# Decoder layer on Trainium2: the feed-forward's row maximum by one reduction over 2048 columns in the next tile, in place of four over 512

## Chip, cores and metric

The kernel runs on one core of one Trainium2 chip. The metric is the device time of one execution in microseconds (us); smaller is better. Where several executions were timed, their median is given.

## What is computed

One decoder layer on 8 sequences of 256 tokens with 512 channels: attention, then a long convolution over a context, then a feed-forward, each on the layer-normalised stream and added to it. The change touches the feed-forward alone, whose weights are 512 x 2048, 512 x 2048 and 2048 x 512:

```python
def activation_quant(x):
    scale = 127.0 / jnp.clip(jnp.max(jnp.abs(x), axis=-1, keepdims=True), EPS, None)
    return jnp.clip(jnp.round(x * scale), -128.0, 127.0) / scale
...
gate = bit_linear(x, w_gate)
up = bit_linear(x, w_up)
activated = up * jnp.square(jax.nn.relu(gate))
activated = subln(activated, subln_weight)      # x * rsqrt(mean(x^2) + 1e-6) * g
return bit_linear(activated, w_down)            # quantises its input's rows to 8 bits
```

`bit_linear` rounds its input, row by row, to integers of -128 to 127, scaled by the greatest absolute value of the row, and its weights to -1, 0, 1. So the 2048 activations of a row have to be finished, weighed by `g`, before their greatest value, and with it the integers for the last product, is known.

## The kernel before

The work has three stages: attention (0 to some 305 us), the convolution (to some 460 us), and the feed-forward, which runs over 16 tiles of 128 rows. Each engine has its own instruction list, in an order written by hand; they meet at semaphores alone. `schedule` (L966) lays out one `turn` per tile: turns 0 to 3 written out, turns 4 to 13 as a loop over pairs, then turns 14 and 15. A turn is a software pipeline. Turn t does the gate and up products of tile t, the end of the scaling and the quantising of tile t-1, the product with `w_down` of tile t-2, and prepares the rows of tile t+2.

The 2048 hidden columns of a tile are done in four chunks of 512 (`IC` = 4). For chunk n of tile t:

- TensorE (L1069) does 4 products for the gate and 4 for the up projection into PSUM;
- ScalarE (`relu`, L1093 and L1095) makes relu(gate) squared;
- VectorE (`chunk`, L1189) multiplies that by the up projection into the small tile `a` (named `toep` in the trace, whose memory it uses again);
- GpSimd (`weigh`, L1306) multiplies by `g` into `act_w` (named `big`), and ScalarE (`square`, L1104) sums the squares of `a`;
- VectorE (`greatest`, L1193) takes the greatest absolute value of the 512 weighed columns into one column of `mb4`.

With all four chunks done, VectorE sums the squares (`scale`, L1199 to L1204), reduces `mb4` to `mb` (L1206), GpSimd raises the variance to -0.5 (`power`, L1302), and VectorE makes the scale `qs` from it (`scale_b`, L1211 to L1219). ScalarE then scales all 2048 columns (`quantise`, L1112), GpSimd makes them integers in bfloat16 (`integers`, L1314), a DMA on SyncE's queue transposes them (L1000), and TensorE multiplies them by `w_down` (L1057); VectorE adds the residual (`final`, L1227).

VectorE's turn also holds the steps of tile t+2: `rows_x2` (L1138, adds the convolution's part to the stream), `rows_stats` (L1143), `rows_mean` (L1148), `rows_var` (L1152), `rows_norm` (L1156), `rows_greatest` (L1160), `rows_scale` (L1164 to L1171), `rows_int` (L1175 to L1179). `rows_stats` and `rows_mean` have an `apart` ahead, an empty instruction between the wait and the work.

What waits for what, in a turn: TensorE's chunk 2 waits for VectorE's chunk 0, its chunk 3 for VectorE's chunk 1, and chunks 0 and 1 of the next tile for VectorE's chunks 2 and 3. ScalarE's `square` of chunk 0 waits until VectorE has summed the squares of the tile before (L1199). ScalarE's order is relu 0, relu 1, square 0, relu 2, square 1, rows_out, relu 3, square 2, quantise (of tile t-1), square 3.

The names of the chunks in what follows: chunk n is VectorE's product of chunk n, L1189, and square n is ScalarE's L1104 of it.

Of the kernel before, what the change touches and what calls it, by code (L numbers as in the profile page):

```python
# [23 lines left out]
ALU = mybir.AluOpType  # L24
ACT = mybir.ActivationFunctionType
AX = mybir.AxisListType
# [5 lines left out]
P = 128  # L32
B, T, C = 8, 256, 512
# [15 lines left out]
NT = B * TT  # L49
# [18 lines left out]
def wait(eng, signal, turn, n):  # L68
    eng.wait_ge(signal.sem, signal.at(turn, n))
# [829 lines left out]
def ffn(nc, ctx, m, g, out, multiply, add_up):  # L899
# [5 lines left out]
    def sb(name, shape, dt=F32):  # L905
        return ctx.enter_context(nc.sbuf_tensor(name, shape, dt))

    def two(name, shape, dt=F32):
        return [sb(f"{name}{r}", shape, dt) for r in range(2)]

    def sig(name, per=1):
        return Signal(ctx.enter_context(nc.semaphore("f_" + name)), per)

    IC = FF // C
# [18 lines left out]
    rl, r2 = ([kv[:, r * C:(r + 1) * C] for r in range(2)] for kv in (kv0, kv1))  # L933
    a = [t[:] for t in toep]
    asq, ss = sb("asq", [P, C]), sb("ss", [P, IC])
    act_w = [m.big[:, 0:FF], m.big[:, FF:2 * FF]]
    act32 = m.big[:, 2 * FF:3 * FF]
    act8 = [y.bitcast(BF16)[:, 0:FF] for y in ys]
    act8t = two("act8t", [P, FK, P], BF16)
    mb4 = sb("mb4", [P, IC])  # L940
    cc, sm, var, r4, cr, mb, bm, rb, qs = (sb(n, [P, 1]) for n in (
        "cc", "sm", "var", "r4", "cr", "mb", "bm", "rb", "qs"))
    fd = two("fd", [P, 1])
# [9 lines left out]
        "turned", "x2", "bn", "mv", "ve", "rs", "xn"))  # L953
    s_mx, s_cl, s_rc, s_s127, s_cx, s_cx2, s_cf = (sig(n) for n in ("mx", "cl", "rc", "s127", "cx", "cx2", "cf"))
    s_x32, s_xq, s_xqt, s_xqe = (sig(n) for n in ("x32", "xq", "xqt", "xqe"))
    s_g, s_u, s_rl, s_r2, s_a, s_as, s_w, s_mb4 = (sig(n, IC) for n in ("g", "u", "rl", "r2", "a", "as", "w", "mb4"))
    s_sm, s_cc, s_var, s_r4, s_mb, s_cr, s_bm, s_rb, s_qs, s_fd = (sig(n) for n in (
        "sm", "cc", "var", "r4", "mb", "cr", "bm", "rb", "qs", "fd"))
    s_a32, s_a8, s_dn, s_fin = (sig(n) for n in ("a32", "a8", "dn", "fin"))
# [172 lines left out]
    def vector(dve):  # L1132
# [3 lines left out]
        def rows_x2(t, bank=TB):  # L1136
            wait(dve, s_turned, t, 1)
            nc.vector.tensor_tensor(row(t), bank, row(t), ALU.add).then_inc(s_x2.sem, 1)  # L1138

        def rows_stats(t):  # L1140
            wait(dve, s_x2, t, 1)
            apart(dve)
            nc.vector.bn_stats(st[:], row(t)).then_inc(s_bn.sem, 1)  # L1143

        def rows_mean(t):
            wait(dve, s_bn, t, 1)
            apart(dve)
            nc.vector.bn_aggr(mv[:], st[:]).then_inc(s_mv.sem, 1)  # L1148

        def rows_var(t):  # L1150
            wait(dve, s_mv, t, 1)
            nc.vector.tensor_scalar(ve[:], mv[:, 1:2], LN_EPS, None, ALU.add).then_inc(s_ve.sem, 1)  # L1152

        def rows_norm(t):
            wait(dve, s_rs, t, 1)
            nc.vector.tensor_scalar(xn, row(t), mv[:, 0:1], rs[:], ALU.subtract, ALU.mult).then_inc(s_xn.sem, 1)  # L1156

        def rows_greatest(t):
            wait(dve, s_xn, t, 1)
            nc.vector.tensor_reduce(mx[:], xn, AX.X, ALU.max, apply_absolute_value=True).then_inc(s_mx.sem, 1)  # L1160

        def rows_scale(t):
            wait(dve, s_mx, t, 1)
            nc.vector.tensor_scalar(cl[:], mx[:], Q_EPS, None, ALU.max).then_inc(s_cl.sem, 1)  # L1164
            wait(dve, s_cl, t, 1)
            nc.vector.reciprocal(rc[:], cl[:]).then_inc(s_rc.sem, 1)
            nc.vector.tensor_scalar(cx[:], cl[:], 1.0 / 127.0, None, ALU.mult).then_inc(s_cx.sem, 1)
            wait(dve, s_rc, t, 1)
            nc.vector.tensor_scalar(s127[:], rc[:], 127.0, None, ALU.mult).then_inc(s_s127.sem, 1)
            wait(dve, s_cx, t, 1)  # L1170
            nc.vector.tensor_scalar(cx2[:], cx[:], cx[:], w3[:], ALU.mult, ALU.mult).then_inc(s_cx2.sem, 1)  # L1171

        def rows_int(t, r):
            wait(dve, s_s127, t, 1)
            nc.vector.tensor_scalar(xq32, xn, s127[:], MAGIC, ALU.mult, ALU.add).then_inc(s_x32.sem, 1)  # L1175
            wait(dve, s_cx2, t, 1)
            nc.vector.tensor_scalar(cf_all[:, bass.ds(t, 1)], cx2[:], cx[:], None, ALU.mult).then_inc(s_cf.sem, 1)
            wait(dve, s_x32, t, 1)
            nc.vector.tensor_scalar(xq[r][:], xq32, -MAGIC, None, ALU.add).then_inc(s_xq.sem, 1)  # L1179

        def chunk(t, n, after=True):
            wait(dve, s_r2, t, n + 1)
            wait(dve, s_u, t, n + 1)
            if n >= 2 or after:

                tp, np_ = (t, n - 1) if n >= 2 else (t - 1, n - 1 + IC)
                wait(dve, s_as, tp, np_)
                wait(dve, s_w, tp, np_)
            nc.vector.tensor_tensor(a[n % 2][:], UB[:, n % 2, :], r2[n % 2][:], ALU.mult).then_inc(s_a.sem, 1)  # L1189

        def greatest(t, n, r):
            wait(dve, s_w, t, n + 1)
            nc.vector.tensor_reduce(mb4[:, n:n + 1], act_w[r][:, n * C:(n + 1) * C], AX.X, ALU.max,  # L1193
                                    apply_absolute_value=True).then_inc(s_mb4.sem, 1)

        def scale(t, r):
            cf = cf_all[:, bass.ds(t, 1)]
            wait(dve, s_as, t, IC)
            nc.vector.tensor_reduce(sm[:], ss[:], AX.X, ALU.add).then_inc(s_sm.sem, 1)  # L1199

            nc.vector.tensor_scalar(cc[:], cf, cf, 1.0 / FF, ALU.mult, ALU.mult).then_inc(s_cc.sem, 1)
            wait(dve, s_cc, t, 1)
            wait(dve, s_sm, t, 1)
            nc.vector.tensor_scalar(var[:], sm[:], cc[:], SUB_EPS, ALU.mult, ALU.add).then_inc(s_var.sem, 1)  # L1204
            wait(dve, s_mb4, t, IC)
            nc.vector.tensor_reduce(mb[:], mb4[:], AX.X, ALU.max).then_inc(s_mb.sem, 1)  # L1206

        def scale_b(t, r):
            cf = cf_all[:, bass.ds(t, 1)]
            wait(dve, s_r4, t, 1)  # L1210
            nc.vector.tensor_scalar(cr[:], r4[:], cf, None, ALU.mult).then_inc(s_cr.sem, 1)  # L1211
            wait(dve, s_mb, t, 1)
            wait(dve, s_cr, t, 1)
            nc.vector.tensor_scalar(bm[:], mb[:], cr[:], Q_EPS, ALU.mult, ALU.max).then_inc(s_bm.sem, 1)
            wait(dve, s_bm, t, 1)
            nc.vector.reciprocal(rb[:], bm[:]).then_inc(s_rb.sem, 1)
            wait(dve, s_rb, t, 1)
            nc.vector.tensor_scalar(qs[:], rb[:], cr[:], 127.0, ALU.mult, ALU.mult).then_inc(s_qs.sem, 1)
            nc.vector.tensor_scalar(fd[r][:], bm[:], m.wmean[:, 2:3], 1.0 / 127.0, ALU.mult, ALU.mult  # L1219
                                    ).then_inc(s_fd.sem, 1)  # L1220

        def final(t, r, stores):
            wait(dve, s_dn, t, 1)
            wait(dve, s_fd, t, 1)
            if stores is not None:
                dve.wait_ge(d_o[r].sem, stores * 16)
            nc.vector.scalar_tensor_tensor(ot[r][:], DB, fd[r][:], row(t), ALU.mult, ALU.add).then_inc(s_fin.sem, 1)  # L1227

        def turn(t, r, after=True, last=True, rows=True, more=True, stored=True, pair=None):
            chunk(t, 0, after)  # L1230
            if not after:
                rows_norm(t + 1)
                rows_greatest(t + 1)
                rows_scale(t + 1)
            if rows:
                rows_x2(t + 2)
            if after:
                greatest(t - 1, 3, 1 - r)
            if rows:
                rows_stats(t + 2)  # L1240
            chunk(t, 1, after)
            if not after:
                rows_int(t + 1, 1 - r)
            if after:
                scale(t - 1, 1 - r)
            if rows:
                rows_mean(t + 2)
            if after:
                scale_b(t - 1, 1 - r)
            if rows:  # L1250
                rows_var(t + 2)
            greatest(t, 0, r)
            chunk(t, 2)
            greatest(t, 1, r)
            if rows:
                rows_norm(t + 2)
            chunk(t, 3)
            if rows:
                rows_greatest(t + 2)
                rows_scale(t + 2)  # L1260
            greatest(t, 2, r)
            if rows:
                rows_int(t + 2, r)
            if last:
                final(t - 2, r, pair - 1 if stored else None)
# [24 lines left out]
        rows_mean(1)  # L1290
        rows_var(1)
        schedule(turn, dve.Fori)
        greatest(NT - 1, 3, 1)
        scale(NT - 1, 1)
        scale_b(NT - 1, 1)
        for t in (NT - 2, NT - 1):
            final(t, t % 2, NT // 2 - 1)

    def gpsimd(pool):
# [38 lines left out]
        integers(NT - 1, 1)  # L1338

    return sync, tensor, scalar, vector, gpsimd  # L1340


# [90 lines left out]
```

## Time and profile before

| what | value |
|---|---|
| median of 3 runs | 678.32 us (677.24 to 678.36) |
| the profiled execution | 679.29 us, its span 677.5 us |
| TensorE busy | 613.7 us, 91% of the span |
| VectorE busy | 485.3 us, 72% |
| ScalarE busy | 455.3 us, 67% |
| GpSimd busy | 269.8 us, 40% |
| mean granted TensorE clock | 0.965 |

The span is the time from the first to the last instruction of the profiled execution; 1.8 us of that execution's time lie around it. Busy shares are means over three stages that are limited by different things, so what the change is worth has to be read in the feed-forward alone, in the last third of the span.

### The profile page before, as it was taken

Reading aid. Unit: us, or ns where it says so; the run is one execution under the profiler, and the core shown is the slowest. Engines: PE = TensorE matmul, PEld = TensorE weight load, DVE = VectorE, ACT = ScalarE, POOL = GpSimd, SP = SyncE. Lnnn points to the kernel's source line nnn. Section 1 sums busy time; section 2 is a strip of 40 time slices with the busy share of each in tenths; the row PEclk is TensorE's granted clock in tenths of the full one; section 3 lists DMA queues with packets and bytes.
Section 4 is the critical chain, followed back from the end, with each engine's and each line's share of the span. In section 5 each row is a group of like instructions: output and inputs, shape, how many; then the busy total and the mean of one; then the engine's idle time right before and its main releaser. Section 6 shows DMA issues by size and latency. Waiting matters only on the chain.

```text
span 677.5 us, 10465 instructions
## 1 busy us (share of the span) xinstructions
PE 613.7 (91%) x2818; PEld 342.0 (50%) x2818; DVE 485.3 (72%) x949; ACT 455.3 (67%) x799; POOL 269.8 (40%) x248
## 2 busy tenths in 40 slices
PE   5889999999999999989999999957799999899975
PEld 4525454535454543367777777743344444444432
DVE  3455767575758372437778877898999999999961
ACT  2363666666666667158988888864778778688771
POOL 1000000100010001137777777742566666666671
PEclk9959999999999997989999999987999999999997
DMA  8473144536261717026555656431042342432424
GB/s 312 126 207 85 40 105 145 122 126 138 110 176 71 208 41 178 24 79 193 169 169 171 192 170 174 156 110 44 16 109 63 82 105 62 106 79 62 94 48 108
DMA packets 75589, 80.89 MB, mean 119 GB/s; under 512 B 38000, under 2 KB 49776, under 8 KB 75440
## 3 DMA queue, kind: packets, MB, share of 16 engines
q1 hardware_dynamic: 75568, 80.65, 43.1%
q8 instruction: 9, 0.15, 0.1%
q14 instruction: 12, 0.10, 0.0%
HBM read 47.51 MB, written 4.28 MB: 76 GB/s over the span
## 4 chain that ended last, share of the span: by engine, by line
PE 26%; DVE 16%; issue 7%; POOL 3%; ACT 2%; DVEq 1%; DMA 1%; ACTq 0%; POOLq 0%; SPq 0%
PE ps L708 20%; DVE toep L1189 3%; PE ps L1069 3%; PE ps L1057 2%; DVE mb L1193 2%; POOL big L1306 2%; DVE ps L1175 1%; DVE ps L1156 1%; DVE mx L1160 1%; DVE qo L761 1%; POOL r L1302 1%; ACT asq L1104 1%; DMA act8t<-ys 1%; ACT kv L1093 1%; DVE x_all L1138 1%
## 5 line engine op out<-in xcount | busy, mean ns | idle before, releaser
L708 PE MATMUL ps<-kv,toep 128*128 128x288 f32 x640 | 157.3, 409 | 1.1 <-PEq L1368 1.1
L708 PEld LDWEIGHTS ps<-kv,toep 128*128 128x128 f32 x640 | 122.3, 192 | 36.1 <-issue 2.4
L1069 PE MATMUL ps<-wt,xqt 128*128 128x512 bf16 x512 | 123.4, 387 | 17.3 <-DVE toep L1189 16.5
L1306 POOL TENSOR_TENSOR big<-toep,wst 128x512 f32<-128x512 f32 x64 | 82.9, 1295 | 41.9 <-DVE toep L1189 41.9
L396 ACT ACTIVATE big<-ps,kscale 128x512 f32<-128x512 f32 x128 | 85.5, 696 | 12.7 <-PE ps L246 10.3
L1069 PEld LDWEIGHTS ps<-wt,xqt 128*128 128x128 bf16 x512 | 48.5, 99 | 79.1 <-DVE toep L1189 24.2
L246 PE MATMUL ps<-qx,kx 128*128 128x512 f32 x128 | 78.3, 633 | 10.5 <-ACT big L396 8.6
L761 DVE TENSOR_REDUCE qo<-big 128x2048 f32 (+1 forms) x32 | 72.2, 2258 | 0.0
L1057 PE MATMUL ps<-wt,act8t 128*128 128x512 bf16 x256 | 60.3, 390 | 7.9 <-DMA act8t<-ys 7.0
L696 POOL TENSOR_TENSOR kv<-ctx 128x768 f32<-128x768 f32 (+1 forms) x32 | 52.7, 1648 | 36.7 <-PE ps L708 27.9
L750 DVE TENSOR_TENSOR big<-ps,qd 128x1024 f32<-128x1024 f32 x32 | 39.2, 1224 | 37.1 <-ACT ys L840 34.6
L1104 ACT ACTIVATE asq<-toep 128x512 f32<-128x512 f32 x64 | 39.5, 618 | 38.8 <-DVE sm L1199 37.4
L217 PE MATMUL ps<-wq_s,xt 128*128 128x512 f32 x128 | 63.4, 593 | 0.8 <-ACT xt L360 0.8
L550 DVE RECIPROCAL yt<-ps 128x512 f32<-128x512 f32 x16 | 53.6, 3349 | 14.4 <-PE ps L264 14.4
L800 POOL TENSOR_TENSOR big<-ys,qd 128x768 f32<-128x768 f32 x32 | 56.6, 1768 | 13.8 <-ACT ys L840 11.7
L284 PE MATMUL ps<-wo_s,yt 128*128 128x512 f32 x128 | 56.6, 594 | 1.0 <-DVE yt L555 1.0
L246 PEld LDWEIGHTS ps<-qx,kx 128*128 128x128 f32 x128 | 25.5, 204 | 46.4 <-ACT big L396 26.2
L646 POOL COPY vo<-vn 128x256 f32<-128x256 f32 x8 | 3.2, 398 | 112.5 <-PE ps L273 86.3
L1189 DVE TENSOR_TENSOR toep<-ps,kv 128x512 f32<-128x512 f32 x64 | 43.5, 679 | 4.7 <-ACT kv L1095 3.4
L1057 PEld LDWEIGHTS ps<-wt,act8t 128*128 128x128 bf16 x256 | 25.2, 100 | 40.9 <-DMA act8t<-ys 8.7
L1193 DVE TENSOR_REDUCE mb<-big 128x1 f32<-128x512 f32 x64 | 43.3, 676 | 0.2 <-POOL big L1306 0.2
L1095 ACT ACTIVATE kv<-kv 128x512 f32<-128x512 f32 x64 | 40.3, 630 | 2.0
(118 smaller groups left out, 958.9 us busy)
## 6 DMA issues: line engine op xcount, KB each, us to landing
qx<-kv SPq DMA_DIRECT2D x128, 128.0 KB, 2.4
wst<-in_wall SPq DMA_DIRECT2D x12, 1024.0 KB, 6.4
wst<-in_wall SPq DMA_DIRECT2D x48, 256.0 KB, 3.7
toep<-krows SPq DMA_DIRECT2D x32, 256.0 KB, 3.7
ctx<-in_ctxt SPq DMA_DIRECT2D x32, 192.0 KB, 2.6
out_y<-ot SPq DMA_DIRECT2D x16, 256.0 KB, 2.9
conv_part<-qo SPq DMA_DIRECT2D x14, 256.0 KB, 2.7
x_all<-in_x SPq DMA_DIRECT2D x2, 1536.0 KB, 14.5
```

The lines of the kernel that those rows point to most:

```text
L217: mm = pe.matmul(bank[:, t, :], xt[:, k, t * P:(t + 1) * P], wq_s[:, k, :], start=(k == 0), stop=(k == CK - 1))
L246: pe.matmul(SB[:, n % 2, :], kx[:, kv, s * P:(s + 1) * P].bitcast(F32R), qx[:, kv, gp * C:(gp + 1) * C].bitcast(F32R), start=True, stop=Tr ...
L284: mm = pe.matmul(OB[:, t, :], yt[:, k, t * P:(t + 1) * P], wo_s[:, k, :], start=(k == 0), stop=(k == CK - 1))
L396: act.activation(pt[:, s, kv, gp * C:(gp + 1) * C], SB[:, n % 2, :], ACT.Exp, scale=kscale[:, c:c + 1]).then_inc(s_e.sem, 1)
L708: mm = pe.matmul(m.ps[:, LB * r + lb, :].rearrange("p (b s) -> p b s", s=WIDE)[:, :, 0:PAIRS], m.toep[r][:, d * P:(d + 1) * P], m.kv[r][:, ...
L761: nc.vector.tensor_reduce(qo[:, :, bass.ds(h * HD, HD)], z[r][:], AX.X, ALU.add).then_inc(s_red.sem, 1)
L800: nc.gpsimd.tensor_tensor(z[r][:, :, :, HD - SHIFTS:HD].rearrange("p n j s -> p n s j"), window(ys[r][:], SHIFTS - 1, (SHIFTS * EW, NB), ( ...
L1057: mm = pe.matmul(DB, act8t[r][:, k, :], down_w[:, k, :], start=(k == 0), stop=(k == FK - 1))
L1069: mm = pe.matmul(bank[:, n % 2, :], xqt[r][:, k, :], wt[:, k, n * C:(n + 1) * C], start=(k == 0), stop=(k == CK - 1))
L1189: nc.vector.tensor_tensor(a[n % 2][:], UB[:, n % 2, :], r2[n % 2][:], ALU.mult).then_inc(s_a.sem, 1)
L1193: nc.vector.tensor_reduce(mb4[:, n:n + 1], act_w[r][:, n * C:(n + 1) * C], AX.X, ALU.max, apply_absolute_value=True).then_inc(s_mb4.sem, 1)
L1306: nc.gpsimd.tensor_tensor(act_w[r][:, n * C:(n + 1) * C], a[n % 2][:], gb[:, n * C:(n + 1) * C], ALU.mult).then_inc(s_w.sem, 1)
```

## The change

The four maxima over 512 columns become one over 2048. It is taken in the turn of the next tile, after the steps `scale`, `rows_mean` and `rows_var` and ahead of `scale_b`. The second reduction from `mb4` to `mb`, the tile `mb4` and its semaphore go. `rows_var` now stands ahead of `scale_b`.

```diff
-        def greatest(t, n, r):
-            wait(dve, s_w, t, n + 1)
-            nc.vector.tensor_reduce(mb4[:, n:n + 1], act_w[r][:, n * C:(n + 1) * C], AX.X, ALU.max,
-                                    apply_absolute_value=True).then_inc(s_mb4.sem, 1)
+        def greatest(t, r):
+            wait(dve, s_w, t, IC)
+            nc.vector.tensor_reduce(mb[:], act_w[r], AX.X, ALU.max, apply_absolute_value=True).then_inc(s_mb.sem, 1)
...
             nc.vector.tensor_scalar(var[:], sm[:], cc[:], SUB_EPS, ALU.mult, ALU.add).then_inc(s_var.sem, 1)
-            wait(dve, s_mb4, t, IC)
-            nc.vector.tensor_reduce(mb[:], mb4[:], AX.X, ALU.max).then_inc(s_mb.sem, 1)
...
             if rows:
                 rows_x2(t + 2)
-            if after:
-                greatest(t - 1, 3, 1 - r)
             if rows:
                 rows_stats(t + 2)
             chunk(t, 1, after)
...
                 scale(t - 1, 1 - r)
             if rows:
                 rows_mean(t + 2)
-            if after:
-                scale_b(t - 1, 1 - r)
             if rows:
                 rows_var(t + 2)
-            greatest(t, 0, r)
+            if after:
+                greatest(t - 1, 1 - r)
+                scale_b(t - 1, 1 - r)
             chunk(t, 2)
-            greatest(t, 1, r)
             if rows:
                 rows_norm(t + 2)
             chunk(t, 3)
             if rows:
                 rows_greatest(t + 2)
                 rows_scale(t + 2)
-            greatest(t, 2, r)
             if rows:
                 rows_int(t + 2, r)
...
         schedule(turn, dve.Fori)
-        greatest(NT - 1, 3, 1)
+        greatest(NT - 1, 1)
         scale(NT - 1, 1)
         scale_b(NT - 1, 1)
```

The other engines' orders are as before. Three places of VectorE's order move.

The first is in the loop, between chunk 0 and chunk 1; `st` are the statistics of tile t+2, REGISTER_ALU rows count the loop's semaphore values. Before:

```order
L1138 TENSOR_TENSOR x_all<-ps,x_all 128x512
L1193 TENSOR_REDUCE mb4<-big 128x1 [waits f_w]
L1143 BN_STATS st<-x_all 128x6 [waits f_x2]
L69 REGISTER_ALU
L1189 TENSOR_TENSOR toep1<-ps,kv1 128x512 [waits f_as,f_w,f_u,f_r2]
```

and with the change:

```order
L1137 TENSOR_TENSOR x_all<-ps,x_all 128x512
L1142 BN_STATS st<-x_all 128x6 [waits f_x2]
L69 REGISTER_ALU
L1188 TENSOR_TENSOR toep1<-ps,kv1 128x512 [waits f_as,f_w,f_u,f_r2]
```

The maximum of the last chunk no longer stands between the sum `x_all` and the statistics that wait for it.

The second is in the loop, between chunk 1 and chunk 2 (`cr` is the first instruction of `scale_b`, `fd` its last, `ve` is `rows_var`). Before:

```order
L1204 TENSOR_SCALAR var<-sm,cc 128x1 [waits f_sm,f_cc]
L1206 TENSOR_REDUCE mb<-mb4 128x1 [waits f_mb4]
L1148 BN_AGGR mv3<-st 128x2 [waits f_bn]
L1211 TENSOR_SCALAR cr<-r4,cf_all 128x1 [waits f_r4]
L1214 TENSOR_SCALAR bm<-mb,cr 128x1 [waits f_cr,f_mb]
L1216 RECIPROCAL rb<-bm 128x1 [waits f_bm]
L1218 TENSOR_SCALAR qs<-rb,cr 128x1 [waits f_rb]
L1219 TENSOR_SCALAR fd0<-bm,wmean 128x1
L1152 TENSOR_SCALAR ve<-mv3 128x1 [waits f_mv]
L1193 TENSOR_REDUCE mb4<-big 128x1 [waits f_w]
L69 REGISTER_ALU
L1189 TENSOR_TENSOR toep0<-ps,kv1 128x512 [waits f_as,f_w,f_u,f_r2]
```

and with the change:

```order
L1202 TENSOR_SCALAR var<-sm,cc 128x1 [waits f_sm,f_cc]
L1147 BN_AGGR mv3<-st 128x2 [waits f_bn]
L1151 TENSOR_SCALAR ve<-mv3 128x1 [waits f_mv]
L1192 TENSOR_REDUCE mb<-big 128x1 [waits f_w]
L1207 TENSOR_SCALAR cr<-r4,cf_all 128x1 [waits f_r4]
L1210 TENSOR_SCALAR bm<-mb,cr 128x1 [waits f_cr,f_mb]
L1212 RECIPROCAL rb<-bm 128x1 [waits f_bm]
L1214 TENSOR_SCALAR qs<-rb,cr 128x1 [waits f_rb]
L1215 TENSOR_SCALAR fd0<-bm,wmean 128x1
L69 REGISTER_ALU
L1188 TENSOR_TENSOR toep0<-ps,kv1 128x512 [waits f_as,f_w,f_u,f_r2]
```

The maximum over 2048 columns now stands between `var` and `cr`, which waits for GpSimd's power of `var`, and `ve` stands right behind the `mv3` that it needs.

The third is the end of VectorE's program, behind chunk 3 of the last tile. Before:

```order
L1189 TENSOR_TENSOR toep1<-ps,kv1 128x512 [waits f_as,f_w,f_u,f_r2]
L1193 TENSOR_REDUCE mb4<-big 128x1 [waits f_w]
L1227 SCALAR_TENSOR_TENSOR ot1<-ps,fd1,x_all 128x512 [waits f_d_o1,f_fd,f_dn]
L1193 TENSOR_REDUCE mb4<-big 128x1 [waits f_w]
L1199 TENSOR_REDUCE sm<-ss 128x1 [waits f_as]
```

and with the change:

```order
L1188 TENSOR_TENSOR toep1<-ps,kv1 128x512 [waits f_as,f_w,f_u,f_r2]
L1223 SCALAR_TENSOR_TENSOR ot1<-ps,fd1,x_all 128x512 [waits f_d_o1,f_fd,f_dn]
L1192 TENSOR_REDUCE mb<-big 128x1 [waits f_w]
L1197 TENSOR_REDUCE sm<-ss 128x1 [waits f_as]
```

There the long maximum stands in the open, ahead of the scaling of the last tile.

## Rows read from the trace of the kernel before

**Rows 1.** One turn of the loop: busy time of each engine, granted clock, DMA.

```profile
core 0: us, PE busy (x) PEld busy (x) DVE busy (x) ACT busy (x) POOL busy (x), PEclk, DMA share, GB/s
582.85:595.18 12.33, 11.36 (x58) 5.31 (x57) 11.54 (x33) 9.50 (x19) 8.15 (x7) 1.00 0.36 85
```

**Rows 2.** Who waited for whom from 508.9 to 620.5 us, nine turns: total, times, longest.

```profile
PE ps L1069 <- DVE toep L1189: 8.7, 18, 0.7
DVE cr L1211 <- POOL r L1302: 4.6, 9, 0.5
```

**Rows 3.** VectorE in order of time, one turn: start us, us, line, operation [idle before].

```profile
576.41 0.68 DVE L1189 TENSOR_TENSOR toep<-ps,kv 128x512 f32<-128x512 f32 x1
...
579.83 0.15 DVE L1206 TENSOR_REDUCE mb<-mb 128x1 f32<-128x4 f32 x1
...
580.57 0.21 DVE L1211 TENSOR_SCALAR cr<-r,cf_all 128x1 f32<-128x1 f32 x1 [0.51 <-POOL r L1302]
...
581.60 0.14 DVE L1152 TENSOR_SCALAR ve<-mv 128x1 f32<-128x1 f32 x1
581.66 0.67 DVE L1193 TENSOR_REDUCE mb<-big 128x1 f32<-128x512 f32 x1
582.25 0.68 DVE L1189 TENSOR_TENSOR toep<-ps,kv 128x512 f32<-128x512 f32 x1
...
588.75 0.68 DVE L1189 TENSOR_TENSOR toep<-ps,kv 128x512 f32<-128x512 f32 x1
```

**Rows 4.** VectorE in order of time, where the convolution ends and the feed-forward starts.

```profile
449.46 0.68 DVE L1138 TENSOR_TENSOR x_all<-ps,x_all 128x512 f32<-128x512 f32 x1
450.25 0.69 DVE L1143 BATCH_NORM_STATS2 st<-x_all 128x6 f32<-128x512 f32 x1
...
452.43 0.16 DVE L1148 BATCH_NORM_AGGREGATE mv<-st 128x2 f32<-128x6 f32 x1
452.65 0.15 DVE L1152 TENSOR_SCALAR ve<-mv 128x1 f32<-128x1 f32 x1
452.76 2.29 DVE L761 TENSOR_REDUCE qo<-big 128x256 f32<-128x2048 f32 x1
454.96 0.80 DVE L1156 TENSOR_SCALAR ps<-x_all,mv,rs 128x512 f32<-128x512 f32 x1
...
467.78 0.69 DVE L1143 BATCH_NORM_STATS2 st<-x_all 128x6 f32<-128x512 f32 x1 [0.49 <-DVE x_all L1138]
```

**Rows 5.** ScalarE in order of time, same turn: square 2, and the next turn's relu 0.

```profile
583.67 0.61 ACT L1104 ACTIVATE asq<-toep 128x512 f32<-128x512 f32 x1
...
587.49 0.63 ACT L1095 ACTIVATE kv<-kv 128x512 f32<-128x512 f32 x1
```

**Rows 6.** The transposing DMA's issue, its landing, and TensorE's first product with it.

```profile
588.58 1.79 SPq L1000 DMA_TRANSPOSE act8t<-ys  x1
...
DMA to landing us min/median/max: 4.3/4.3/4.3
...
593.60 3.62 PE L1057 MATMUL ps<-wt,act8t 128*128 128x512 bf16 x16
```

**Rows 7.** The last two turns and the end, each engine in order of time.

```profile
638.06 0.68 DVE L1189 TENSOR_TENSOR toep<-ps,kv 128x512 f32<-128x512 f32 x1
...
653.49 0.68 DVE L1189 TENSOR_TENSOR toep<-ps,kv 128x512 f32<-128x512 f32 x1
...
646.00 7.07 PE L1069 MATMUL ps<-wt,xqt 128*128 128x512 bf16 x32
...
663.66 6.01 PE L1057 MATMUL ps<-wt,act8t 128*128 128x512 bf16 x16 [6.57 <-DMA act8t<-ys]
670.61 3.61 PE L1057 MATMUL ps<-wt,act8t 128*128 128x512 bf16 x16 [0.94 <-DVE ot L1227]
...
654.49 0.61 ACT L1104 ACTIVATE asq<-toep 128x512 f32<-128x512 f32 x1
...
665.08 1.77 SPq L1000 DMA_TRANSPOSE act8t<-ys  x1
```

More of the change, by code:

```diff
@@ L939, in ffn @@
     act8t = two("act8t", [P, FK, P], BF16)
-    mb4 = sb("mb4", [P, IC])
     cc, sm, var, r4, cr, mb, bm, rb, qs = (sb(n, [P, 1]) for n in (
@@ L955, in ffn @@
     s_x32, s_xq, s_xqt, s_xqe = (sig(n) for n in ("x32", "xq", "xqt", "xqe"))
-    s_g, s_u, s_rl, s_r2, s_a, s_as, s_w, s_mb4 = (sig(n, IC) for n in ("g", "u", "rl", "r2", "a", "as", "w", "mb4"))
+    s_g, s_u, s_rl, s_r2, s_a, s_as, s_w = (sig(n, IC) for n in ("g", "u", "rl", "r2", "a", "as", "w"))
     s_sm, s_cc, s_var, s_r4, s_mb, s_cr, s_bm, s_rb, s_qs, s_fd = (sig(n) for n in (
```

## The prediction

> **What bounds the kernel now.** The change touches only the feed-forward, so I first looked for a stretch of it that repeats. In the loop a turn takes 12.33 us, with VectorE busy for 11.54, TensorE for 11.36, ScalarE for 9.50 and GpSimd for 8.15, at the full granted clock [rows 1]. Two engines are near the limit, so the waits have to decide. Over nine turns TensorE stands still 8.7 us, always for VectorE's chunks (18 waits, two a turn: 0.7 and, from the rest, (8.7 - 9 x 0.7) / 9 = 0.27 us). VectorE itself waits for one thing only, GpSimd's power, 4.6 / 9 = 0.51 us a turn [rows 2]. VectorE's order in time shows the rest as an unbroken row [rows 3]. So VectorE's list sets the turn and TensorE has 0.97 us of slack: what is taken off VectorE shortens the turn, until another loop closes. Turns 2 to 13, twelve of them, have this full form. Turn 14 begins at 638.06; from 646.00 TensorE runs 7.07 us of gate and up products with no wait [rows 7], so turns 14 and 15 are TensorE's, and the end is a chain of its own.
>
> One thing about reading VectorE: the durations overlap. A maximum over 512 starts at 581.66, is shown with 0.67 us, and the next operation starts at 582.25 [rows 3]. What an operation costs the queue is the distance between starts, 0.59 us. I count in those.
>
> **The change, per turn of the loop (VectorE).**
>
> 1. Four maxima over 512 go: 4 x 0.59 = 2.36 us off [rows 3].
> 2. One over 2048 comes. The trace has no such maximum, but a reduction over the same 2048 columns at the convolution's end: 452.76 to the next start at 454.96, 2.20 us [rows 4]. Its bounds are 2.20 and, if the long one were worth four short ones, 2.36. I take 2.20: same engine, same amount read from the same memory.
> 3. `mb` from `mb4`, and the wait for the power. Before, `mb` starts at 579.83 and `cr` at 580.57, so 0.74 us hold `mb`, the mean and 0.51 of standing still [rows 3]. Now mean, `ve` and then the long maximum stand there. From mean to `ve` is 0.22, from `ve` to the next 0.11 [rows 4], together 0.33. The 2.20 us behind it cover the power altogether. That is 0.41 off; and `ve` loses its old place, 581.60 to 581.66 [rows 3], another 0.06.
> 4. The cover over `rows_stats` is gone. A maximum stood between the sum and the statistics that wait for it. Where the two stand together, the starts are 0.79 apart (449.46, 450.25) and not 0.59: 0.20 added. Once, the statistics came after an idle 0.49 [rows 4], which would be 0.57 added. I take 0.20, since that pair too has nothing but the empty instruction between; 0 and 0.57 are the ends.
> 5. The maxima behind chunk 2 and ahead of `rows_int` covered nothing that is late: their neighbours' inputs are made several instructions earlier. If one of them was needed after all, it costs what step 4 does, 0.20 us.
>
> Sum: -2.36 + 2.20 - 0.41 - 0.06 + 0.20 = -0.43 us, a turn of 11.90.
>
> The Trainium skill (VectorE: DVE Perf Modes, The DRAIN you can't avoid) says that after each VectorE operation the pipe is flushed and the next doesn't start before it is empty. By that, whole durations would count, and the merging itself would save far more than the 0.16 us of steps 1 and 2. The rows speak against it, since starts are closer than durations [rows 3].
>
> **Do the others keep up?** Chunk 2 gets later: it started 5.84 us after chunk 0 [rows 3], and now 5.84 - 2 x 0.59 + 0.20 - 0.41 - 0.06 + 2.20 = 6.59. Behind it hangs ScalarE's square 2, which held the queue until relu 0 of the next tile was done: 583.67 to 587.49 + 0.63 = 588.12, 4.45 us without a gap [rows 5]. So the next chunk 0 can't come before 6.59 + 0.68 + 0.05 + 4.45 + 0.05 = 11.82. That is just inside 11.90. ScalarE becomes nearly as critical as VectorE, and no more than 0.1 us is left before it decides.
>
> TensorE: its wait for chunk 1 goes (0.27), that for chunk 0 shrinks, 11.36 busy fits in 11.90. The DMA: its issue stood 588.58 - 576.41 = 12.17 after chunk 0, it lands 4.3 later, and the product that needs it began at 593.60, 17.19 after [rows 3, 6]. Square 2, and so quantise, integers and issue, now come at 6.59 + 0.73 = 7.32 where they were at 7.26, so the data lands at 16.53, and the product is ready at 17.19 - 0.43 - 0.27 = 16.49. Some 0.04 us of wait, inside TensorE's slack of half a microsecond.
>
> **Times twelve:** -5.2 us. SyncE's and GpSimd's orders are untouched.
>
> **The ends.** Turn 0 has one maximum between chunk 3 and the next chunk 0: -0.6 (its ends: 0 and -0.6). Turn 1 lacks `final`, and the ScalarE chain of 11.8 us takes its gain away: 0. Turn 14: TensorE's, 0, perhaps +0.1 for the DMA. Turn 15: chunk 1 is set by TensorE; chunk 2, before at 653.49, comes 2.20 - 0.74 - 0.59 = 0.87 later, 654.36, and square 2 at 655.09 instead of 654.49: 0.6 later [rows 7]. Quantise, integers, DMA and TensorE's product of tile 14 (663.66, it waited 6.57 for that DMA) all hang behind it: +0.6. The last tile's own maximum stands in the open, 2.20 for 0.59: 1.6 later. Before, its DMA was issued at 665.08 and landed at about 669.4, while TensorE's last product started at 670.61 behind the last but one [rows 7]. Landing at 671.0 against 671.2: hidden, barely; if not, 0.1 to 0.5 more. I take +0.7 for the end.
>
> **Sum.** -5.2 - 0.6 + 0.7 = -5.1 us, on the profiled execution's 679.29 (span 677.5 and 1.8 around it) 674.2. That execution lies 1.0 above the median of 678.32; against the median, 673.2.
>
> **The rivals.**
>
> A. The long maximum costs what four short ones do, and only the covered wait is won: -0.27 a turn, 12 x 0.27 = 3.2, with the ends 3.1: 675.2. Against it: 2.20 in rows 4. For it: the operation there isn't a maximum. The Trainium skill (VectorE: DVE Perf Modes, Rules for kernel authors) speaks so: don't fuse chained operations for speed, since the flush comes anyway. Chance 0.12.
>
> B. The statistics stand idle each time as at 467.78 [rows 4]: 0.37 more a turn, so -0.06 x 12 = -0.7, with the ends -0.6: 677.7, no change that can be told. That idle time occurred once, in code that had run for the first time, and at 449.46 it didn't. Chance 0.12.
>
> C. Slower: ScalarE takes over. If chunk 2 comes more than 12.33 - 5.23 = 7.10 us after chunk 0, square 2, quantise, square 3 and relu 0 make the turn longer than before, and VectorE waits ahead of chunk 0. It stands at 6.59, so 0.5 us is missing: step 4 at its upper end (0.37) and 0.2 more, from the register instruction and four waits that now come right behind `fd` with nothing to hide them. A turn at 12.40 gives 12 x 0.07 + 0.7 = +1.5, or 679.8. For it: it is the one chain that the change lengthens and doesn't shorten. Against it: it needs two misfortunes. Chance 0.07.
>
> D. More than forecast: no cost in step 4 and the -0.6 on top, with ScalarE's chain then as the floor: about -0.6 a turn, 12 x 0.6 + 0.6 - 0.3 = 7.5, or 670.8. Chance 0.06.
>
> The forecast holds 0.63; by itself it would reach from 671.5 to 674.8.
>
> **How the numbers follow.** A measurement of this kernel can tell about 0.2% from no change, 1.36 us, so faster means below 676.96. The forecast, A and D are faster: 0.81. B: 0.12 within. C: 0.07 slower. The range reaches from D to B, 670.8 to 677.7; outside lie C and the edges.
>
> **What would show it.** VectorE's starts of chunk 0 in the loop 11.90 apart, ScalarE's turn with almost no idle time between square 2 and the next relu 0; no wait of `cr` for the power; the start after the long maximum 2.20 behind it; statistics 0.79 behind the sum; chunk 2 6.6 behind chunk 0; TensorE's waits for chunks down from 0.97 to about 0.5 a turn. At the end, TensorE's product of tile 14 0.6 later, counted from turn 14's chunk 0, and the last one with no wait for its DMA. I am wrong if the turn stays at 12.3 though `cr` doesn't wait, if ScalarE's square 2 is what ends the idle time of the chain (C), or if the statistics wait about half a microsecond (B).

## The result, and the profile after

The changed kernel takes 673.98 us (median of 4, 673.66 to 674.68) against 678.34 for the kernel before on the same chip (4 runs): a ratio of 0.9942, with a 95% interval of 0.9926 to 0.9958. It is faster by 4.4 us, where 5.1 were forecast. The profiled execution took 673.91 us, with a span of 672.1.

One turn of the loop (a turn is from chunk 0 to the next chunk 0), which answers to [rows 1]; the columns are those given there:

```profile
570.80:582.71 11.91, 11.46 (x57) 5.23 (x56) 11.49 (x29) 9.69 (x19) 8.20 (x8) 1.00 0.37 88
```

Who waited for whom from 499.6 to 606.45, nine turns, which answers to [rows 2]: total, times, longest.

```profile
ACT asq L1103 <- DVE sm L1197: 16.7, 9, 1.9
PE ps L1068 <- DVE toep L1188: 3.4, 8, 0.5
ACT asq L1103 <- DVE toep L1188: 2.5, 9, 0.3
```

TensorE's waits for chunks fell from 8.7 to 3.4 us, `cr` no longer waits for the power in the loop at all, and a new line stands there: ScalarE's square 2 waits for VectorE's chunk 2, 0.3 us a turn. That is the chain of rival C, now in touch: square 2 starts 0.73 us after chunk 2's start, where it was 1.42. In ScalarE's order of time:

```profile
578.04 0.63 ACT L1103 ACTIVATE asq<-toep 128x512 f32<-128x512 f32 x1 [0.27 <-DVE toep L1188]
```

Over turns 2 to 13, from chunk 0 at 487.77 to chunk 0 at 630.13, a turn takes 11.86 us; before it was 12.33.

VectorE in order of time in that turn, which answers to [rows 3]:

```profile
570.80 0.68 DVE L1188 TENSOR_TENSOR toep<-ps,kv 128x512 f32<-128x512 f32 x1
571.40 0.68 DVE L1137 TENSOR_TENSOR x_all<-ps,x_all 128x512 f32 x1
572.18 0.69 DVE L1142 BATCH_NORM_STATS2 st<-x_all 128x6 f32 x1
...
573.69 0.21 DVE L1202 TENSOR_SCALAR var<-sm,cc 128x1 f32<-128x1 f32 x1
573.82 0.17 DVE L1147 BATCH_NORM_AGGREGATE mv<-st 128x2 f32<-128x6 f32 x1
574.03 0.15 DVE L1151 TENSOR_SCALAR ve<-mv 128x1 f32<-128x1 f32 x1
574.10 2.28 DVE L1192 TENSOR_REDUCE mb<-big 128x1 f32<-128x2048 f32 x1
576.29 0.20 DVE L1207 TENSOR_SCALAR cr<-r,cf_all 128x1 f32<-128x1 f32 x1
...
577.31 0.69 DVE L1188 TENSOR_TENSOR toep<-ps,kv 128x512 f32<-128x512 f32 x1
...
582.71 0.69 DVE L1188 TENSOR_TENSOR toep<-ps,kv 128x512 f32<-128x512 f32 x1
```

The long maximum costs 576.29 - 574.10 = 2.19 us, the statistics start 0.78 behind the sum, mean to `ve` to the maximum is 0.28, and chunk 2 stands 6.51 behind chunk 0: forecast were 2.20, 0.79, 0.33 and 6.59.

The last two turns and the end are not as forecast. TensorE in order of time, which answers to [rows 7], then SyncE's issue of the transposing DMA of tile 12, then the DMA view of 630 to 638 us with the instruction loads and the median time from issue to landing:

```profile
632.83 1.89 PE L1068 MATMUL ps<-wt,xqt 128*128 128x512 bf16 x8
636.55 3.63 PE L1056 MATMUL ps<-wt,act8t 128*128 128x512 bf16 x15 [1.84 <-DMA act8t<-ys]
640.02 7.07 PE L1068 MATMUL ps<-wt,xqt 128*128 128x512 bf16 x32
...
658.68 5.63 PE L1056 MATMUL ps<-wt,act8t 128*128 128x512 bf16 x15 [8.14 <-DMA act8t<-ys]
665.24 3.61 PE L1056 MATMUL ps<-wt,act8t 128*128 128x512 bf16 x16 [0.94 <-DVE ot L1223]
```

```profile
630.47 2.34 SPq L999 DMA_TRANSPOSE act8t<-ys  x1
```

```profile
q8 instruction: 1, 0.02, 0.8%
q14 instruction: 1, 0.01, 0.4%
...
act8t<-ys SPq DMA_TRANSPOSE x1, 6.0
```

The DMA landed 6.0 us after its issue, not 4.3, and TensorE stood still for 1.84 us in a stretch in which nothing gives that back. (A row with x15 lacks one of the product's 16 records.)

The account, profile against profile (679.29 and 673.91, 5.4 apart):

| stretch | before | after | difference | forecast |
|---|---|---|---|---|
| start to chunk 0 of tile 0 | 463.81 | 462.35 | -1.5 | 0 |
| turn 0 | 14.55 | 13.72 | -0.8 | -0.6 |
| turn 1 | 11.74 | 11.70 | 0.0 | 0 |
| turns 2 to 13 | 147.96 | 142.36 | -5.6 | -5.2 |
| chunk 0 of tile 14 to chunk 1 of tile 15 | 12.03 | 13.97 | +1.9 | 0 |
| from there to the end | 27.41 | 28.00 | +0.6 | +0.7 |

The first line belongs to code that the change doesn't touch. It is the scatter of single executions: chunk 0 of tile 0 lay between 461.4 and 464.3 in the profiles of the ten kernels below, in no order. So the feed-forward gained 3.9 us in these profiles; the medians of the whole kernel lie 4.4 apart.

### The profile page after: what moved, and what is told of

Its sections match the earlier page's. It is cut to its first block, busy times and chain, and to the rows that moved or that the text cites. A ratio compares the mean times of both kernels' runs of the same rounds, so it can differ in the third digit from the quotient of the medians.

```text
span 672.1 us, 10384 instructions
## 1 busy us (share of the span) xinstructions
PE 609.0 (91%) x2801; PEld 339.8 (51%) x2818; DVE 483.4 (72%) x885; ACT 456.4 (68%) x799; POOL 269.1 (40%) x248
## 4 chain that ended last, share of the span: by engine, by line
PE 24%; DVE 19%; issue 6%; ACT 3%; DMA 2%; POOL 1%; DVEq 1%; ACTq 0%; POOLq 0%; SPq 0%
PE ps L708 21%; DVE mb L1192 5%; DVE toep L1188 4%; PE ps L1056 2%; DMA act8t<-ys 2%; DVE x_all L1137 1%; ACT asq L1103 1%; PE ps L1068 1%; DVE ps L1155 1%; DVE qo L761 1%; DVE mx L1159 1%; DVE ot L1223 1%; ACT big L1111 1%; ACT kv L1094 1%; POOL ys L1306 1%
## 5 line engine op out<-in xcount | busy, mean ns | idle before, releaser
L1068 PE MATMUL ps<-wt,xqt 128*128 128x512 bf16 x497 | 120.6, 386 | 11.1 <-DVE toep L1188 9.1
L800 POOL TENSOR_TENSOR big<-ys,qd 128x768 f32<-128x768 f32 x32 | 56.4, 1762 | 13.6 <-ACT ys L840 11.5
L1092 ACT ACTIVATE kv<-ps 128x512 f32<-128x512 f32 x64 | 37.4, 584 | 7.1 <-PE ps L1068 7.1
L411 ACT ACTIVATE osq<-ps 128x512 f32<-128x512 f32 x16 | 9.6, 598 | 47.5 <-PE ps L284 47.5
```

The costliest lines, as they stand in the source:

```text
L800: nc.gpsimd.tensor_tensor(z[r][:, :, :, HD - SHIFTS:HD].rearrange("p n j s -> p n s j"), window(ys[r][:], SHIFTS - 1, (SHIFTS * EW, NB), ( ...
L1068: mm = pe.matmul(bank[:, n % 2, :], xqt[r][:, k, :], wt[:, k, n * C:(n + 1) * C], start=(k == 0), stop=(k == CK - 1))
```

## The experiments

Each kernel was compared with the kernel before on the same chip. All change VectorE's program alone, but for the ninth. Turns are meant over tiles 2 to 13.

**1. The changed kernel again (control).**

> The changed kernel once more. In its first profile the loop's turns took 11.86 us (forecast 11.90), but in turn 14 TensorE's down product of tile 12 waited 1.84 us for the transposing DMA, which landed 6.0 us after its issue and not 4.3, with a 16 KB instruction load on another DMA queue in front of its last packets. Theory 1 (a coincidence of the two transfers, which belongs to that place of the program): the same again, landing near 6.0, 674.0 us. Theory 2 (chance of that execution): landing at 4.3 to 4.7, and the profiled execution near 672.3. Turns of 11.86 in both.

Measured: 674.41 us (10 runs, ratio 0.9940, 0.9926 to 0.9955), turns of 11.87, and the late DMA again: landing at 6.1, TensorE waiting 1.94 us. So it comes back with this program and isn't the chance of one execution.

**2. The power's wait bare again.** `cr` is taken out of `scale_b` into a function of its own, `scale_cr`, and stands ahead of the long maximum:

```diff
             if after:
+                scale_cr(t - 1)
                 greatest(t - 1, 1 - r)
                 scale_b(t - 1, 1 - r)
```

> The one long maximum stays, but cr, which waits for GpSimd's power, now stands ahead of it, so the wait is bare again. My theory (most of the gain is that the wait is covered): the turn grows by 0.47 idle + 0.13 for cr - 0.18 behind the maximum = 0.42, to 12.28 us, and the time by 12 x 0.42 = 5.0 to about 679; no more than 0.1 a turn is left of the change. Rival (the merging of four into one is what pays): no idle time to speak of matters, 674 to 675.

Measured: 680.78 us (10 runs, ratio 1.0032, 1.0015 to 1.0049), turns of 12.28. VectorE in order of time:

```profile
579.11 0.21 DVE L1202 TENSOR_SCALAR var<-sm,cc 128x1 f32<-128x1 f32 x1
...
579.99 0.21 DVE L1207 TENSOR_SCALAR cr<-r,cf_all 128x1 f32<-128x1 f32 x1 [0.39 <-POOL r L1298]
580.12 2.28 DVE L1192 TENSOR_REDUCE mb<-big 128x1 f32<-128x2048 f32 x1
582.43 0.21 DVE L1212 TENSOR_SCALAR bm<-mb,cr 128x1 f32<-128x1 f32 x1
```

One instruction moved by one place gives back 0.41 of the 0.47 us a turn. With the late DMA and the longer end on top, the merged maximum without the cover makes a slower kernel. The rival "merging is what pays" has fallen. The turn came out as forecast; the total was 1.8 above, since the forecast had counted the wait in turns 2 to 13 alone: in the profiles turn 1 took 0.4 us more as well (12.11 for 11.70) and the end 1.2 (29.2 for 28.0).

**3. Four short maxima, the last of them over the power.** The kernel before, with the reduction from `mb4` to `mb` in a function of its own, `row_max`, and:

```diff
-            if after:
-                greatest(t - 1, 3, 1 - r)
             if rows:
                 rows_stats(t + 2)
...
             if rows:
                 rows_mean(t + 2)
-            if after:
-                scale_b(t - 1, 1 - r)
             if rows:
                 rows_var(t + 2)
+            if after:
+                greatest(t - 1, 3, 1 - r)
+                row_max(t - 1)
+                scale_b(t - 1, 1 - r)
```

> The kernel before with four maxima of 512, of which only the last is moved behind var, mean and ve, where it covers the power; the reduction from mb4 to mb stays. My theory: 1.19 from var to cr in place of 0.87 and of the maximum's 0.59, -0.27; -0.06 for ve; +0.19 for the statistics, which lose their cover: -0.14 a turn, 12.19 us, about 676.6. Rival (merging pays, the cover doesn't): the statistics' 0.19 alone, 12.5 a turn, 680 or no gain.

Measured: 675.82 us (10 runs, ratio 0.9961, 0.9947 to 0.9975), turns of 12.21, most at 12.18.

```profile
578.45 0.68 DVE L1193 TENSOR_REDUCE mb<-big 128x1 f32<-128x512 f32 x1
579.16 0.16 DVE L1208 TENSOR_REDUCE mb<-mb 128x1 f32<-128x4 f32 x1
579.24 0.20 DVE L1213 TENSOR_SCALAR cr<-r,cf_all 128x1 f32<-128x1 f32 x1
```

Even 0.7 us of cover swallows the power; the small reduction is the one that now waits, for the maximum in front of it. A reordering without any merging wins 2.8 us, where the changed kernel wins 4.2 on the same chip (experiment 1). In the loop it wins less of it, 1.5 us of 5.6 in the profiles. Another 0.9 came behind chunk 0 of tile 14, mostly because TensorE's product of tile 14 took 5.13 us for 6.01, at a mean granted clock of 0.70 for 0.60 of full; from one profile that part can't be put down to the order.

Experiments 2 and 3 take the change apart. Both, and the changed kernel, pay the statistics' 0.19 us a turn. If the parts add up, this is what each is worth. The merging without the cover wins 0.05 a turn net of that, so it is worth 0.24 by itself (0.17 for the maxima, the rest for the second reduction); the cover by a short maximum wins 0.12 to 0.15 net, so 0.31 to 0.34; the cover by the long one is worth 0.41. And 0.24 + 0.41 - 0.19 = 0.46, against the 0.47 measured.

**4. The long maximum early**, between the sum and the statistics:

```diff
             if rows:
                 rows_x2(t + 2)
+            if after:
+                greatest(t - 1, 1 - r)
             if rows:
                 rows_stats(t + 2)
...
             if after:
-                greatest(t - 1, 1 - r)
                 scale_b(t - 1, 1 - r)
```

> The one long maximum, but at the place of the old fourth one, between the sum and the statistics, ahead of chunk 1. If VectorE's own list were all that counts: 12.33 - 2.36 - 0.06 + 2.19 = 12.10 a turn and about 676. My theory (two chains stand close behind it: ScalarE's square 0 waits for the sum of squares behind chunk 1, and its queue then runs 8.8 us without a gap to the next chunk 0): chunk 1 comes 1.6 later, the sum of squares 4.58 after chunk 0, so the turn is 4.58 + 8.77 = 13.35 us; with turns 1, 14 and 15 hit as well some 692 us, slower than before.

Measured: 694.66 us (4 runs, ratio 1.0233, 1.0206 to 1.0261), turns of 13.42 on average, 13.33 and 13.53 in turn. VectorE, and ScalarE's square 0 in the same turn:

```profile
583.82 0.69 DVE L1188 TENSOR_TENSOR toep<-ps,kv 128x512 f32<-128x512 f32 x1 [0.26 <-ACT kv L1094]
...
588.40 0.15 DVE L1197 TENSOR_REDUCE sm<-ss 128x1 f32<-128x4 f32 x1
...
597.34 0.69 DVE L1188 TENSOR_TENSOR toep<-ps,kv 128x512 f32<-128x512 f32 x1 [0.44 <-ACT kv L1094]
```

```profile
588.67 0.63 ACT L1103 ACTIVATE asq<-toep 128x512 f32<-128x512 f32 x1 [3.74 <-DVE sm L1197]
```

Theory said 13.35, and that holds to 0.1. The same instructions, 2% slower: the sum of squares comes 4.58 after chunk 0, ScalarE idles 3.74 us for it, and then VectorE waits for ScalarE. For a 2.2 us instruction the place matters more than its length.

**5. The last two gaps covered too.** The changed kernel, with `scale_cr` as in experiment 2 and:

```diff
                 rows_x2(t + 2)
-            if rows:
-                rows_stats(t + 2)
             chunk(t, 1, after)
...
                 scale(t - 1, 1 - r)
             if rows:
+                rows_stats(t + 2)
+            if after:
+                greatest(t - 1, 1 - r)
+            if rows:
                 rows_mean(t + 2)
+            if after:
+                scale_cr(t - 1)
             if rows:
                 rows_var(t + 2)
             if after:
-                greatest(t - 1, 1 - r)
                 scale_b(t - 1, 1 - r)
```

> The changed kernel with its last two gaps of VectorE covered: the statistics go behind var (half a microsecond behind the sum they need), and mean, cr and ve stand behind the long maximum, so that neither waits for its neighbour. My theory (VectorE's list sets the turn): -0.19 for the statistics, about -0.15 for mean, cr and ve: a turn of about 11.5 in place of 11.86, -4.3 us, near 670. ScalarE's chain moves along with chunk 2 (6.1 + 5.2 = 11.3) and allows it. Rival (the others are the bound now: TensorE is busy 11.36 of a turn and its down product waits for a DMA that lands 16.5 after chunk 0): turns of 11.7 or more, 672 to 674, with TensorE waiting for the DMA.

Measured: 668.13 us (4 runs, ratio 0.9841, 0.9818 to 0.9864), turns of 11.53.

```profile
570.73 2.27 DVE L1192 TENSOR_REDUCE mb<-big 128x1 f32<-128x2048 f32 x1
572.92 0.17 DVE L1147 BATCH_NORM_AGGREGATE mv<-st 128x2 f32<-128x6 f32 x1
573.01 0.18 DVE L1207 TENSOR_SCALAR cr<-r,cf_all 128x1 f32<-128x1 f32 x1
573.12 0.15 DVE L1151 TENSOR_SCALAR ve<-mv 128x1 f32<-128x1 f32 x1
573.29 0.21 DVE L1212 TENSOR_SCALAR bm<-mb,cr 128x1 f32<-128x1 f32 x1
```

The loop's part came as forecast. In the profiles 2.2 us more came from turn 0 (11.48 for 13.72), and 0.4 from turn 1. In turn 0 the statistics with their longer idle time [rows 4] stood ahead of tile 1's integers, for which TensorE waits there; now the integers start 1.2 us earlier. The other half is TensorE's clock. TensorE around these integers in the changed kernel, and the stretch in which its granted clock is 0.50, the lower level of 1.2 GHz (the columns are those of [rows 1]); then TensorE in this experiment, and its whole turn 0:

```profile
469.05 0.61 PE L1046 MATMUL ps<-identb,xq 128*128 128x128 bf16 x4 [2.92 <-DVE xq L1178]
469.45 4.90 PE L1068 MATMUL ps<-wt,xqt 128*128 128x512 bf16 x16
468.60:472.00 3.40, 2.95 (x10) 1.31 (x11) 2.09 (x5) 1.18 (x2) 2.19 (x3) 0.50 0.00 0
...
469.82 0.40 PE L1046 MATMUL ps<-identb,xq 128*128 128x128 bf16 x4 [1.76 <-DVE xq L1178]
470.06 3.62 PE L1068 MATMUL ps<-wt,xqt 128*128 128x512 bf16 x16
464.28:475.76 11.48, 9.67 (x51) 4.57 (x49) 11.05 (x28) 8.55 (x19) 5.74 (x5) 1.00 0.11 32
```

TensorE idles 1.76 us ahead of the integers and not 2.92, its clock doesn't fall there, and the product behind them takes 3.62 us for 4.90. The profiles of experiments 5, 8 and 9, which share this order, have no such stretch in turn 0; the other nine all do. So about half of what turn 0 gives is the clock and not VectorE's list.

**6. Chunk 2 late.** The changed kernel with:

```diff
-            chunk(t, 2)
             if rows:
                 rows_norm(t + 2)
+            chunk(t, 2)
             chunk(t, 3)
```

> The changed kernel with chunk 2 and rows_norm exchanged: VectorE's list is as long as before, but chunk 2 starts about 7.2 after chunk 0 and not 6.5. My theory (ScalarE's chain from square 2 to the next relu 0 takes 5.2 from chunk 2's start and lies just behind VectorE's own): turns of 7.2 + 5.2 = 12.4 us, +0.55 x 12 = +6.7, near 681, with VectorE waiting for ScalarE ahead of chunk 0. If VectorE's list alone sets the turn: 11.86 and 674.

Measured: 683.67 us (5 runs, ratio 1.0064, 1.0043 to 1.0085), turns of 12.50. From 505 to 620 us VectorE, which waited for nobody in the changed kernel's loop, waits:

```profile
ACT asq L1103 <- DVE toep L1188: 8.8, 9, 1.0
DVE toep L1188 <- ACT kv L1094: 5.6, 9, 0.7
```

VectorE's work is unchanged; chunk 2 starts 7.22 after chunk 0, and 7.22 + 5.2 = 12.4 (measured 12.43 and 12.61 in turn). So the second chain is real, 0.7 us of delay to chunk 2 turned a gain into a loss, and rival C would have come true had chunk 2 slipped by another half a microsecond. The total is 2.7 above the forecast of 681: turns 1 and 14 pay too (12.41 and 14.07, for 11.70 and 12.25 in the changed kernel), and behind the wait for its late DMA TensorE's granted clock was 0.71 of full on average, with a product of 5.31 us there instead of 3.63.

**7. VectorE's program padded** at its start:

```diff
+        for _ in range(23):
+            apart(dve)
         dve.wait_ge(d_x0.sem, 16)
```

> The changed kernel with 23 empty instructions at VectorE's start, where it waits for the first input anyway, so that its feed-forward loop ends at the same place of its program as in the kernel before. Three kernels with the shorter VectorE program had a DMA that landed 6.0 us after its issue in turn 13, each with an 8 KB instruction load 1.5 us after the issue; the kernel before and the one with four maxima had neither. Theory 1 (the load, whose moment hangs on the program's length, makes the landing late): no such load there, landing at 4.3 to 4.7, TensorE's down product in turn 14 without the 1.9 us of waiting, 672.3. Theory 2 (the late landing comes from the turn's new timing): 674.2 as before.

Measured: 675.22 us (5 runs, ratio 0.9943, 0.9923 to 0.9964), the landing again at 6.0, TensorE waiting 1.78, and the 8 KB load again 0.7 us after the issue (the expectation puts this load at 1.5; around tile 12's DMA the late kernels' traces have it at 0.7 to 1.0). Where VectorE's program ends its loop isn't what makes the DMA late. My first theory of it fell, as far as this padding tests it: the load stayed where it was.

**8. Both ends.** As 5, with:

```diff
-            if after:
+            if after and more:
                 greatest(t - 1, 1 - r)
...
+            if more and not rows:
+                greatest(t, r)
             if last:
...
-        greatest(NT - 1, 1)
         scale(NT - 1, 1)
+        greatest(NT - 1, 1)
```

> As e5, and the ends: the maximum of tile 14 is taken at the end of turn 14, where VectorE waits 3.3 us for TensorE, and that of tile 15 behind var, over the power. My theory: chunk 2 and square 2 of turn 15 come 0.4 us earlier than in e5 (then ScalarE's own order holds them), and so do quantise, DMA and both last products: -0.4 to -0.9 against e5, 669.3. Rival (the end hangs on the transposing DMA of tile 14 in a way that VectorE doesn't reach): the same as e5.

Measured: 668.10 us (4 runs, ratio 0.9845, 0.9824 to 0.9866): no different from 5. In the profiles the last stretch, from chunk 0 of tile 15 on, fell from 29.8 to 28.7 us. Half of that is the order: the DMA of tile 14 was issued 0.55 us earlier after that chunk. The other half is TensorE's product of tile 14, here for experiment 5 and then for this one (each row lacks one record, by the landing the first); the mean granted clock over it was 0.59 and 0.64 of full:

```profile
653.92 5.72 PE L1056 MATMUL ps<-wt,act8t 128*128 128x512 bf16 x15 [8.12 <-DMA act8t<-ys]
...
653.21 5.17 PE L1056 MATMUL ps<-wt,act8t 128*128 128x512 bf16 x15 [7.56 <-DMA act8t<-ys]
```

In this execution a second DMA landed late as well, that of tile 2, issued at the start of turn 4, and turns 4 and 5 took 1.5 us more together (12.20 and 12.47; in experiment 5 they took 11.43 and 11.73). What the median would be without such landings isn't known.

**9. The down product of tile 12 later.** As 8, with TensorE taking it behind chunks 0 and 1 of tile 15, and `final` of tile 12 behind the variance of tile 14:

```diff
+                if n == 1 and not more:
+                    down(t - 3, 1 - r, pair)
...
-            if last:
+            if last and (rows or not more):
                 down(t - 2, r, pair if stored else 1, first=not stored and r == 0)
```

> As e8, and TensorE takes the down product of tile 12 behind gate and up chunks 0 and 1 of tile 15, not ahead of them, with VectorE's final of tile 12 moved behind it. My theory (in turn 14 TensorE stood still 1.8 us for the DMA that lands 6.0 after its issue, and chunk 1 of tile 15, which starts the chain of the end, stood behind that product): the wait is hidden, chunk 1 of tile 15 comes some 2.5 us earlier, and so does the end, 665.5. Rival (the end hangs on something else, the product's own time counts in either place): 668 as e8.

Measured: 666.58 us (4 runs, ratio 0.9821, 0.9805 to 0.9838), the fastest of all. TensorE in turns 14 and 15:

```profile
630.96 3.61 PE L1068 MATMUL ps<-wt,xqt 128*128 128x512 bf16 x16 [1.52 <-DVE toep L1190]
634.41 3.62 PE L1056 MATMUL ps<-wt,act8t 128*128 128x512 bf16 x16
...
651.05 5.37 PE L1056 MATMUL ps<-wt,act8t 128*128 128x512 bf16 x16 [6.12 <-DMA act8t<-ys]
657.85 3.63 PE L1056 MATMUL ps<-wt,act8t 128*128 128x512 bf16 x16 [1.43 <-DMA act8t<-ys]
```

Chunk 1 of tile 15 came 2.3 us earlier (11.64 after chunk 0 of tile 14, for 13.92; 2.5 were forecast), but the end only 1.0 (39.9 after that chunk, for 40.9): the last product now waits for the last tile's DMA. The chain that had been hidden became the bound. In place of the DMA, TensorE waits 1.52 us for VectorE's chunk. The forecast of 665.5 was 1.1 too low.

**10. The last maximum behind the variance**, and nothing else (one run):

```diff
         schedule(turn, dve.Fori)
-        greatest(NT - 1, 1)
         scale(NT - 1, 1)
+        greatest(NT - 1, 1)
         scale_b(NT - 1, 1)
```

> The changed kernel with the sum of squares and the variance of the last tile ahead of its long maximum, so that this covers the power there too. Forecast in the prediction: the 1.6 us that the last maximum adds are hidden, since the last product waits for the last but one. If so, the last tile's DMA is issued about 1 us earlier and the last product starts no earlier, counted from the last but one: 674. If the last tile's DMA was what it waited for, the end comes up to 1 us earlier.

Measured: 673.18 us; from chunk 0 of tile 14 to the end 42.0 us, as in the changed kernel. My 1 us was wrong: the sum of squares has to wait for ScalarE's square 3, so the last DMA was issued only 0.1 us earlier.

```profile
651.61 0.16 DVE L1197 TENSOR_REDUCE sm<-ss 128x1 f32<-128x4 f32 x1 [1.09 <-ACT asq L1103]
```

With a shift of 0.1 us the run can't tell a hidden DMA from one that is waited for. What shows the hiding is the changed kernel's own trace, below under "The end".

## Why the prediction was right, and where it wasn't

**What bounds the kernel**: right. What was taken off VectorE's list came off the turn, in four different orders, to 0.1 us (12.28, 12.21, 11.86, 11.53; forecast 12.28, 12.19, 11.90, 11.5).

**Steps 1 and 2** (2.36 off, 2.20 on): 2.19. A reduction of another kind over as many columns was the right row to take. Whole durations would have given 4 x 0.67 - 2.28 = 0.40 us for the merging, and rival A gives nothing for it; by the starts it is 0.17. Both passages that the prediction takes from the Trainium skill say more than it used. The section "The DRAIN you can't avoid" of "VectorE: DVE Perf Modes" adds that a next operation that isn't held starts earlier. With that the trace agrees: independent operations start 0.59 apart at a duration of 0.67 [rows 3]. And the row against fusing under "Rules for kernel authors" on the same page goes on to ask for fewer operations, so it is no support for rival A.

**Step 3**, the covered wait, is the larger part of the gain: experiment 2 takes it away and 0.41 us a turn goes with it; experiment 3 has the cover without the merging and keeps 0.12 to 0.15. 0.28 us instead of the 0.33 for mean and `ve` is most of what was left over (0.47 a turn measured, 0.43 forecast).

**Step 4** (0.20 for the statistics): 0.19, in every turn but one. The 0.49 us of idle time behind the sum [rows 4] came back in turn 0, at the same place (0.47), so it belongs to that place; rival B was rightly small. That step 5 cost nothing fits the turn's sum; no run has it alone.

**Do the others keep up**: forecast were 11.82 for ScalarE's chain against 11.90 for VectorE's, and square 2 now waits 0.3 us for chunk 2. TensorE's waits for chunks came down to 0.38 us a turn, where about 0.5 was forecast. Experiments 4 and 6 show the chain from both of its ends. It was nearer than a reader of busy shares would think: ScalarE was busy 9.5 of 12.3 us.

**Turn 0**: -0.8 for -0.6. The interval from chunk 3 to the next chunk 0 shrank by 0.6, as forecast. Chunk 3 itself, which waits for ScalarE and TensorE there, came 0.2 us earlier; TensorE's product ahead of it took 4.90 us for 5.13, both partly at the lower clock.

**The wrong step** is "Turn 14: TensorE's, 0, perhaps +0.1 for the DMA". It cost 1.9 us. I had taken 4.3 us for the landing, since the three turns I had looked at all showed it [rows 6]. Over all sixteen the greatest was 4.7 before and 6.0 after, and for this very transfer, tile 12's, it was 4.6 before. There TensorE began the product 4.63 us after the issue with no idle time; now it was ready 4.2 us after the issue. So some 0.3 us of waiting would have come even with the old landing, and the rest is the late one. The calculation had even found the margin gone (ready at 16.49, landing at 16.53), and priced a later landing at nothing beyond that. TensorE's half microsecond of slack covers a landing a few tenths late in the loop; nothing does in turn 14, and a landing 1.7 us late isn't covered in the loop either (experiment 8, turns 4 and 5).

**The end**: +0.6 for +0.7. The last tile's maximum stayed hidden: its DMA was issued at 660.35 and landed 4.3 us later, at 664.6. The last product started at 665.24 and waited, as before, 0.94 us for VectorE's `ot` of tile 14 and for no DMA.

```profile
660.35 1.77 SPq L999 DMA_TRANSPOSE act8t<-ys  x1
```

**The sum**: turns 0 and 2 to 13 gave 0.6 us more than forecast, turn 14 took 1.9 that I had not priced, the end 0.1 less. That makes 1.2 us too much gain in the forecast for the feed-forward by the profiles, and 0.7 by the medians, of which the difference is the scatter of the first line of the table. That the profiled execution, 673.91 us, lies so near to the 674.2 forecast for it is luck in part: the 1.5 us ahead of the feed-forward made up for most of turn 14.

## What to carry to other kernels

Cost the list of an engine that works in order by the distances between starts, and look for the instructions that are short but wait: a long instruction with nothing to wait for belongs over them. Before moving it, follow every chain that hangs on what now comes later, as a sum of its own in the same turn, and take the loop and the turns behind it apart: what has half a microsecond of slack in one has none in the other. Compare the granted clock of a stretch before a gain in it is put down to the order. A transfer whose margin comes out near zero has to be priced with its slowest landing.

## What was not expected of the hardware

The same transposing DMA landed 4.2 to 4.7 us after its issue nearly always, and after 6.0 or 6.1 for tile 12 (issued at the start of turn 14) in eight of the eleven changed profiles (the changed kernel and experiments 1, 2, 5, 6, 7, 8 and 10), once more in experiment 8 for tile 2. In each of these cases the trace's DMA records have a load of 16 KB of instructions, on another queue, that starts 3.9 to 4.0 us after the issue and takes 0.9 to 1.2 us. In experiments 4 and 9 that load starts 4.7 and 6.7 us after the issue of tile 12's DMA, and the landing is 4.3 and 4.5.

But a load at 3.9 to 4.0 isn't enough: the kernel before and experiment 3 have it there for tile 12, experiments 5, 9 and 10 for tile 2, and these five landed at 4.4 to 4.6. The records tell the two kinds apart. Each DMA raises its semaphore in sixteen steps, and it has landed with the last of them. In the changed kernel fifteen steps of tile 12's came 4.4 to 4.6 us after the issue, and one at 6.03. The same records have 32 packets of 4 bytes around the end of this transfer. In the five cases that landed in time all 32 lie before the load's start; in the nine late ones two or four lie behind it, two of them directly at the load's end, and only one of the sixteen steps is late. And in all fourteen the next DMA, the store of `out_y`, has one late step as well, 1.3 to 1.7 us behind its other fifteen. So such a load goes with one late step in sixteen, and the transposing DMA has it when its last packets aren't out as the load starts; in the kernel before they were out 0.01 us earlier. The packets are told apart here by their size alone, since the records don't name their transfer.

Whose instructions they are, and what sets the moment of the load, isn't shown: padding VectorE's program didn't move the load, another order on TensorE did (experiment 9), and so did the slower turns of experiment 4. The 8 KB load 0.7 to 1.0 us after the issue, which I had blamed first, is missing in experiment 8's second case and present in experiment 9 (0.7) without harm.
